# A transformer block with a mixture of experts: two thirds of the shared expert moved ahead of the experts, with the routing done at once beside it

## The chip, the cores and the metric

One Trainium2 chip, one of its cores. The metric is the device time of one execution in microseconds; several executions are taken, and their median counts. A core has five engines with instruction queues of their own: TensorE (PE: matmuls, and weight loads PEld), VectorE (DVE), ScalarE (ACT), GpSimd (POOL) and SyncE (SP, which here only issues DMAs). They wait for each other by semaphores. An engine works through its queue in order, so whatever stands behind a waiting instruction waits too.

## What is computed

The input is 32 blocks of 256 tokens with 256 features. A token mixer with a layer norm gives `h`; one class token is put ahead of each block (so 32 x 257 rows); attention with 16 heads is added. The change is in what comes then, a gated feed-forward with a shared expert of 1024 hidden columns and eight routed experts of 256, of which each row takes two:

```python
xf = layernorm(h).reshape(-1, 256)
shared = silu(xf @ shared_w1.T) * (xf @ shared_w2.T) @ shared_w3.T
scores = sigmoid(xf @ router_w.T)
_, top_idx = top_k(scores + expert_bias, 2)
gates = scores * one_hot(top_idx, 8).sum(axis=-2)
h12 = einsum('td,ehd->teh', xf, w12); h1, h2 = split(h12, 2, axis=-1)
routed = einsum('teh,edh->td', silu(h1) * h2 * gates[:, :, None], w3)
return h + (shared + routed)
```

## The kernel before

**Stage A** (`stage_a`, one block of instructions) does mixer and attention, unrolled by batch and software-pipelined over 16 places n of a step. Its `ffn_stats` (lines 812 to 825) takes mean and variance of each finished block of rows for the last layer norm into `mv3`; the blocks themselves go to `hscr` in DRAM. At the very end DVE adds epsilon to all 66 columns (L973) and POOL takes the power -0.5 of them at once (L1049).

**Stage B** (`stage_b`) is three blocks of instructions, each ended by a barrier of all engines. Rows are held as K = 33 blocks of two tiles of 128 rows (32 blocks, and one with the 32 class rows).

*Routing* goes over the 33 blocks. Per block: SP loads `hb` (L1175, L1178); DVE normalises (`norm`, L1158); PE transposes (`turn`, L1204); ACT and DVE split z into a high and a low part (L1249, L1338), since products are made of three fp32r terms; PE makes the logits with matmuls of 8 columns (`router`, L1216); ACT takes Tanh (L1253); DVE ranks the eight scores, picks two and makes the gates (`scores`, L1272 to L1292); PE counts the rows before each row (`counts`, L1226 to L1230); DVE turns that into two row numbers (`places`, L1299 to L1334); POOL writes the normalised rows to these places of `zs` with four indirect DMAs (L1433). Every expert has a region of `zs` large enough for all rows. The first 12 blocks also carry the weights: load (L1173), copy to fp32r on ACT (L1258, `whi`), subtraction on POOL (L1427, `wlo`), through two buffers. After the last block DVE makes the lists of tiles and moves all row numbers (L1375 to L1420), and POOL writes the rows of zeros that fill each expert's last tile (L1440).

*Experts* goes over NT = 140 tiles of 128 gathered rows. SP loads a tile from `zs` (L1473, its row number read from a table) and stores the result to `ys` (L1481); the four other engines are pipelined over three tiles.

*Shared expert* goes over the 33 blocks in a loop of two. Per block: z again from `hscr`, then four times (u = 0 to 3) `hidden` (24 matmuls of 256 columns, L1656), Silu (L1696), product (L1729), `head` and `split` into high and low parts (L1703, L1735), and, one u later, `output` (12 matmuls, L1670), with `turn` of the next block at u = 2. The block's sum is added to `h` (L1751); four indirect DMAs of POOL gather its expert rows from `ys` (L1790), DVE adds them times their gates (L1756), and SP stores the output (L1624).

Of the kernel before, what the change touches and what calls it, by code (L numbers as in the profile page):

```python
# [15 lines left out]
F32 = mybir.dt.float32  # L16
# [7 lines left out]
D = C * H  # L24
P = 128
# [43 lines left out]
def stage_a(nc, ctx, sem, a, hscr, mv3, rs3, eye, mhalf, ps):  # L69
# [55 lines left out]
    mh65 = sb("mh65", [P, (B + 1) * LT])  # L125
# [64 lines left out]
    wo_in, wos_ok, vb_ok, vb_in, roh_ok = sem("wo_in"), sem("wos_ok"), sem("vb_ok"), sem("vb_in"), sem("roh_ok")  # L190
# [8 lines left out]
    pcr_ok, pc_ok = sem("pcr_ok"), sem("pc_ok")  # L199
# [139 lines left out]
    def _(pe):  # L339
# [244 lines left out]
        pe.wait_ge(spread_ok, 1)  # L584
        pe.wait_ge(ones_in, 16 * 2 * 2)
        pe.wait_ge(vb_in, 16 * 3)
        pe.wait_ge(wos_ok, 1)
# [136 lines left out]
    def _(dve):  # L724
# [89 lines left out]
        def ffn_stats(b):  # L814
# [4 lines left out]
            dve.wait_ge(ln3, b * 5 + 2)  # L819
# [3 lines left out]
            dve.wait_ge(ln3, b * 5 + 4)  # L823
# [41 lines left out]
        dve.memset(mh65[:], -0.5)  # L865
# [67 lines left out]
        for n in range(2):  # L933
            for f in range(FT):
# [14 lines left out]
                          ALU.subtract).then_inc(wos_ok, 1)  # L949
# [20 lines left out]
        dve.wait_ge(ln3, 5 * B + 1)  # L970
        dve.bn_aggr(mv3[:, B * LT, :], st3[:, 0, :]).then_inc(ln3, 1)
        dve.wait_ge(ln3, 5 * B + 2)
        dve.tensor_scalar(rs3[:], mv3[:, :, 1], EPS, None, ALU.add).then_inc(ln3, 1)  # L973
# [3 lines left out]
    def _(pool):  # L977
# [68 lines left out]
        for j in range(B + 2):  # L1046
            batch(j, j)
        pool.wait_ge(ln3, 5 * B + 3)
        pool.tensor_tensor(rs3[:], rs3[:], mh65[:], ALU.pow)  # L1049


def stage_b(nc, ctx, sem, a, out, hscr, mv3, rs3, eye, ps):

# [12 lines left out]
    REG = K * L + P  # L1066
    NT = (TOP * K * L + NE * (P - 1)) // P + 1
    assert NT % 2 == 0
    UW = FT * 2 * UH + 2 * D
    ONE = LT * NE  # L1070
    zs = nc.dram_tensor("zs", [NE * REG, D], F32, kind="Internal").ap()
    ys = nc.dram_tensor("ys", [NT * P, D], F32, kind="Internal").ap()

    whi = sb("whi", [P, NU, UW], F32R)
    wlo = sb("wlo", [P, NU, UW], F32R)
    rwr = sb("rwr", [P, FT * NE])
    rwh = sb("rwh", [P, FT, NE], F32R)
    rwl = sb("rwl", [P, FT, NE], F32R)
    ebias = sb("ebias", [P, ONE])
    before = sb("before", [P, ONE, NE])  # L1080
    earlierf = sb("earlierf", [P, P])
    earlier = sb("earlier", [P, P], F32R)
    ones = sb("ones", [P, P], F32R)
    region = sb("region", [P, ONE])
    rowid = sb("rowid", [P, 1])
    tileid = sb("tileid", [1, NT])
    hb = [sb("hb%d" % p, [P, LT, D]) for p in range(2)]
    z3 = [sb("z3_%d" % p, [P, LT, D]) for p in range(3)]
# [4 lines left out]
    uu = sb("uu", [P, 3, 2 * L])  # L1093
    raw2 = sb("raw2", [P, UW])
    RAW = 2
    raw = [uu[:].rearrange("p a b -> p (a b)"), raw2[:]]
    assert UW == 3 * 2 * L
# [3 lines left out]
    th = sb("th", [P, ONE])  # L1101
    sc = sb("sc", [P, ONE])
    key = sb("key", [P, ONE])
    gt = sb("gt", [P, ONE, NE])
    eq = sb("eq", [P, ONE, NE])
    rank = sb("rank", [P, ONE])
    gate = sb("gate", [P, ONE])
    mask = sb("mask", [P, ONE], F32R)
    filled = sb("filled", [P, ONE])
    slot = sb("slot", [P, ONE])  # L1110
    smax = sb("smax", [P, LT])
    ssum = sb("ssum", [P, LT])
    hit = sb("hit", [P, TOP, ONE])
    two = sb("two", [P, LT, TOP])
    idx = [sb("idx%d" % p, [P, LT * TOP], I32) for p in range(3)]
    slots = sb("slots", [P, K * LT * TOP])
    offset = sb("offset", [P, K * LT * TOP])
    moved = sb("moved", [P, K * LT * TOP])
    shift = sb("shift", [P, NE])
    idxs = sb("idxs", [P, K * LT * TOP], I32)  # L1120
    gates = sb("gates", [P, K * LT * TOP])
    gnow = sb("gnow", [P, LT * TOP])
    tail = sb("tail", [P, NE], I32)
    tailf = sb("tailf", [P, NE])
    rows = sb("rows", [1, NT], I32)
# [744 lines left out]
```

## Time and profile before

| | us |
|---|---|
| median of the runs shown | 2719.99 (2716.59 to 2720.41, 3 runs) |
| the profiled execution | 2719.27, its span 2717.4 |
| busy: PE, PEld | 2368.3, 1952.8 |
| busy: DVE, ACT, POOL | 1541.2, 1023.1, 696.2 |
| mean granted clock of TensorE | 0.915 |

Busy time is summed by engine over the span. Matmuls are pipelined, so a busy PE is not PE at its peak. The granted clock is the share of 2.4 GHz that TensorE was given; it has two levels, 2.4 and 1.2 GHz (1.00 and 0.50), and a window that lies across a switch shows a mean.

### The profile page before, as it was taken

To read this page: it belongs to the slowest core of one execution; us is meant where nothing else is said; L and a number is where in the kernel's file an instruction comes from. 1 tells how busy PE (TensorE), PEld (TensorE's weight loads), DVE (VectorE), ACT (ScalarE), POOL (GpSimd) and SP (SyncE) were. 2 spreads that over 40 slices of the span, in tenths; PEclk is the share of its full clock that TensorE was granted. 3 is DMA by queue.
4 is the path that set the end of the run, shared out by engine and by line. 5 is a ranking of instruction groups with operands and counts; after the bars stand their busy time and mean duration, and the time that the engine had idled before them with its cause. 6 is when DMAs were issued, how large, how long until landed. Compare 5 with 4: busy or idle time off the path is not lost. (4 is left out here: it accounts for less than half of the span.)

```text
span 2717.4 us, 47912 instructions
## 1 busy us (share of the span) xinstructions
PE 2368.3 (87%) x15654; PEld 1952.8 (72%) x15655; DVE 1541.2 (57%) x3820; ACT 1023.1 (38%) x2129; POOL 696.2 (26%) x775
## 2 busy tenths in 40 slices
PE   3789999999999999998735674999999899999999
PEld 3567777677766777776424563777777799999999
DVE  5356666666666666665248886333443355555554
ACT  0144444444544454444412111444444233333332
POOL 2232223322332233221037654000000122222222
PEclk9689999999999999999755555999999999999999
DMA  2333322333233323333025332222222122222111
GB/s 69 44 52 72 66 57 58 72 66 64 52 71 71 67 51 64 73 58 57 16 77 165 121 116 85 85 85 85 85 87 85 47 62 62 62 62 60 58 57 54
DMA packets 136380, 190.30 MB, mean 70 GB/s; under 512 B 24323, under 2 KB 96021, under 8 KB 136261
## 3 DMA queue, kind: packets, MB, share of 16 engines
q1 hardware_dynamic: 123204, 153.06, 24.1%
q0 software_dynamic: 13056, 35.67, 4.0%
q8 instruction: 73, 1.20, 0.2%
q14 instruction: 47, 0.38, 0.1%
HBM read 82.06 MB, written 54.03 MB: 50 GB/s over the span
## 5 line engine op out<-in xcount | busy, mean ns | idle before, releaser
L793 DVE TENSOR_REDUCE mx<-ps 128x2 f32<-128x514 f32 x512 | 351.1, 686 | 219.4 <-PE ps L448 219.3
L633 ACT ACTIVATE pT<-ps 128x514 f32<-128x514 f32 x512 | 307.0, 600 | 377.7 <-PE ps L465 373.4
L448 PE MATMUL ps<-km,q 112*128 112x258 f32 x1024 | 265.0, 341 | 91.3 <-DVE mx L793 79.3
L448 PEld LDWEIGHTS ps<-km,q 112*128 112x128 f32 x1024 | 164.0, 193 | 188.0 <-DVE mx L793 140.3
L465 PE MATMUL ps<-q,km 114*128 114x258 f32 x1024 | 233.6, 310 | 12.4 <-ACT pT L633 8.8
L1786 POOL TENSOR_TENSOR mark<-rowid 128x1 f32<-128x1 f32 x33 | 6.4, 194 | 854.2 <-DVE idx L1742 854.2
L1656 PE MATMUL ps<-zhi,whi 128*128 128x256 f32 x1056 | 214.4, 285 | 1.5 <-DVE zlo L1724 1.5
L1656 PE MATMUL ps<-zhi,wlo 128*128 128x256 f32 x1056 | 211.1, 281 | 0.0
L1656 PE MATMUL ps<-zlo,whi 128*128 128x256 f32 x1056 | 210.7, 281 | 0.0
L465 PEld LDWEIGHTS ps<-q,km 114*128 114x128 f32 x1024 | 164.9, 196 | 61.2 <-issue 31.1
L996 POOL TENSOR_TENSOR nb<-mv,mneg 128x2 f32<-128x2 f32 x32 | 6.2, 195 | 737.8 <-DVE rs L756 737.8
L1729 DVE TENSOR_TENSOR uu<-ps,sil 128x512 f32<-128x512 f32 x132 | 91.1, 690 | 157.8 <-ACT sil L1696 138.5
L1696 ACT ACTIVATE sil<-ps 128x512 f32<-128x512 f32 x132 | 78.9, 598 | 259.2 <-PE ps L1656 259.2
L1656 PEld LDWEIGHTS ps<-zhi,whi 128*128 128x128 f32 x1056 | 163.2, 190 | 1.9 <-ACT zhi L1707 1.9
L1656 PEld LDWEIGHTS ps<-zhi,wlo 128*128 128x128 f32 x1056 | 163.0, 189 | 0.0
L1656 PEld LDWEIGHTS ps<-zlo,whi 128*128 128x128 f32 x1056 | 162.5, 189 | 0.0
L482 PE MATMUL ps<-pT,va 128*32 128x257 f32 x2048 | 146.3, 399 | 0.0
L1735 DVE TENSOR_TENSOR hlo<-uu,hhi 128x512 fp32r<-128x512 f32 x132 | 91.4, 692 | 92.2 <-ACT hhi L1703 91.5
L1790 POOL DMA_INDIRECT raw<-ys,idx x132 | 130.8, 991 | 38.1 <-issue 33.5
L1595 DVE TENSOR_TENSOR uu<-ps,sil 128x256 f32<-128x256 f32 x140 | 59.5, 425 | 142.8 <-ACT sil L1576 142.8
L1433 POOL DMA_INDIRECT zs<-z,idx x132 | 128.2, 971 | 35.3 <-issue 34.9
L734 DVE RECIPROCAL rden<-ps 128x256 f32<-128x256 f32 x64 | 112.0, 1752 | 30.2 <-PE ps L372 30.2
(326 smaller groups left out, 5459.5 us busy)
## 6 DMA issues: line engine op xcount, KB each, us to landing
z<-zs SPq DMA_DIRECT2D x140, 128.0 KB, 2.0
ys<-z SPq DMA_DIRECT2D x140, 128.0 KB, 1.8
hb<-hscr SPq DMA_DIRECT2D x66, 256.0 KB
q<-qhi SPq DMA_DIRECT2D x128, 129.0 KB, 4.2
km<-khi SPq DMA_DIRECT2D x256, 64.5 KB, 3.3
xs<-in_x SPq DMA_DIRECT2D x64, 256.0 KB, 4.6
hscr<-h SPq DMA_DIRECT2D x34, 256.0 KB, 5.1
q<-qlo SPq DMA_DIRECT2D x64, 129.0 KB, 5.1
```

The source lines that it names most:

```text
L448: last = pe.matmul(ps[:, k, 0:NP], q2[p % U][0:MAXROW, QAT[g], t * P:(t + 1) * P], km[p % 2][0:MAXROW, k, g, :], start=True, stop=True)
L465: pe.matmul(ps[:, 4 + k, 0:NP], km[p % 2][0:MAXROW + 2, k, g, t * P:(t + 1) * P], q2[p % U][0:MAXROW + 2, QAT[g], :], start=True, stop=Tru ...
L482: last = pe.matmul(ps[SLOT * j:SLOT * (j + 1), 7, 0:N], va[p % 2][:, t, h, :], pT[:, h, t, :], start=False, stop=(t == LT - 1), skip_group ...
L633: act.activation(pT[:, 2 * g:2 * g + 2, t, :], ps[:, 4:6, 0:N], ACT.Exp, scale=HD ** -0.5).then_inc(s_ok, 1)
L734: dve.reciprocal(rden[:, f, :], ps[:, 3, f * L:(f + 1) * L]).then_inc(y_step, 1)
L793: dve.tensor_reduce(mx[:, t, 2 * QAT[g]:2 * QAT[g] + 2], ps[:, 0:2, 0:N], AX_X, ALU.max, negate=True).then_inc(mx_ok, 1)
L1433: pool.indirect_dma_start(zs, bass.IndirectOffsetOnAxis(idx[p][:, at:at + 1], 0), z3[p][:, t, :], None).then_inc(zs_out[p], 16)
L1656: last = pe.matmul(ps[:, 2 * (u % 2) + c, m * L:(m + 1) * L], w_[:, u, at:at + P], z_[:, f, :], start=(n == 0), stop=(n == len(mm) - 1))
L1696: act.activation(sil[:, u % 2, :].rearrange("p (c l) -> p c l", c=2), ps[:, 2 * (u % 2):2 * (u % 2) + 2, 0:L], ACT.Silu).then_inc(sil_ok, 1)
L1729: dve.tensor_tensor(uu[:, u % 2, :].rearrange("p (c l) -> p c l", c=2), ps[:, 2 * (u % 2):2 * (u % 2) + 2, L:2 * L], sil[:, u % 2, :].rear ...
L1735: dve.tensor_tensor(hlo[:, u % 2, :], uu[:, u % 2, :], hhi[:, u % 2, :], ALU.subtract).then_inc(hlo_ok, 1)
L1790: pool.indirect_dma_start(yg[:, t, c, :], None, ys, bass.IndirectOffsetOnAxis(idx[0][:, at:at + 1], 0)).then_inc(y_in, 16)
```

## The change

Three things are changed, which the diff below shows in its core.

In stage A, `ffn_stats` now also adds epsilon for its block (one more DVE operation), and POOL takes the root of these two columns in the new `ffn_root`, four batches later in its list; only two columns are left for the end.

Stage B keeps three blocks of instructions, with other contents. The *first* computes the shared expert of 22 of the 33 blocks (XN), unrolled. Beside blocks 0 to 10 it also normalises, transposes and splits the 22 other blocks, two per block (`norm_x`, `turn_x`, `high_x`, `low_x`), makes the logits of all 33, and stores every normalised block to DRAM (`zd`). The weights of the eight experts are loaded at the ends of blocks 0 to 7. Beside blocks 11 to 15 DVE routes all rows at once with operations 520 columns wide (`route`), cut into pieces placed after each u. POOL then writes the tails and all scatters, each from one of three buffers that SP fills from `zd` (`load_s`). The sum of shared expert and h goes back to `hscr` (`store_acc`). Row numbers are now final when they are made, so `zs` is compact. The *second* is the expert stage as before, over NT = 136 tiles; SP's row number is the tile's. The *third* is the shared expert of the 11 last blocks, unrolled, with the gathers and combines of all 33 blocks, three per block, through two buffers (the 32 class rows apart).

```diff
 def ffn_stats(b):
+            dve.tensor_scalar(rs3[:, bass.ds(b * LT, LT)], mvb[:, :, 1], EPS, None, ALU.add).then_inc(ln3, 1)
...
+        def ffn_root(b):
+            pool.wait_ge(ln3, b * 6 + 6)
+            pool.tensor_tensor(rs3[:, bass.ds(b * LT, LT)], rs3[:, bass.ds(b * LT, LT)], mhalf[:], ALU.pow)
         def batch(j, p):
             if has(j + 1):
                 split_x(j + 1, p + 1)
+            if has(j - 4):
+                ffn_root(j - 4)
...
-        pool.tensor_tensor(rs3[:], rs3[:], mh65[:], ALU.pow)
+        pool.tensor_tensor(rs3[:, B * LT:], rs3[:, B * LT:], mhalf[:], ALU.pow)
...
-    NT = (TOP * K * L + NE * (P - 1)) // P + 1
+    NT = (TOP * (B * L + B) + NE * (P - 1)) // P
+    X1 = K // 3
+    XN = 2 * X1
+    NX = 3
...
+            def load_s(s):
+                if s >= NX:
+                    sp.wait_ge(zs_out[s % NX], 16 * LT * TOP * (s // NX))
+                sp.dma_start(zx[s % NX][:], zd[s]).then_inc(zx_in[s % NX], 16)
...
+            for k in range(XN):
+                if k > 0:
+                    store_acc(sp, k - 1)
+                    if k < XN - 1:
+                        load_h(sp, k + 1)
+                if k < X1:
...
+                elif k == X1:
...
+                    for s in range(NX):
+                        load_s(s)
+                elif k >= X1 + 3:
+                    per = -(-(K - NX) // (XN - X1 - 3))
+                    for s in range(NX + per * (k - X1 - 3), min(K, NX + per * (k - X1 - 2))):
+                        load_s(s)
+            store_acc(sp, XN - 1)
...
+            for k in range(XN):
+                for u in range(NS):
+                    hidden(pe, k, u)
+                    if u >= 1:
+                        output(pe, k, u - 1)
+                    elif k > 0:
+                        output(pe, k - 1, NS - 1)
+                    if k < X1:
+                        if u == 0:
+                            logits(k, k % 2)
+                            turn_x(2 * k)
+                        if u == 1:
+                            logits_x(2 * k)
+                            turn_x(2 * k + 1)
+                        if u == 2:
+                            logits_x(2 * k + 1)
+                    if u == 2 and k < XN - 1:
+                        turn(pe, k + 1)
+                if k == X1 + 1:
+                    places()
...
+            def route(k, u):
+                if (k, u) == (X1, 1):
+                    keys()
+                if (k, u) == (X1, 2):
+                    best(0)
+                if (k, u) == (X1, 3):
+                    single(0)
...
+                if (k, u) == (X1 + 1, 2):
+                    single(1)
+                    masks()
...
+                if (k, u) == (X1 + 3, 0):
+                    tables()
+                if (k, u) == (X1 + 3, 1):
+                    positions()
+                if (k, u) == (X1 + 3, 2):
+                    slots(0)
+                    slots(1)
...
+                if (k, u) == (X1 + 4, 1):
+                    lists()
...
+            def scatter(s):
+                b = s % NX
+                pool.wait_ge(zx_in[b], 16 * (held[b] + s // NX + 1))
+                pool.tensor_tensor(mark[:, s:s + 1], rowid[:], rowid[:], ALU.add)
+                rows = P if s < B else B
+                for t in range(LT if s < B else 1):
                     for c in range(TOP):
+                        pool.indirect_dma_start(zs, bass.IndirectOffsetOnAxis(idxs[0:rows, s * LT + t, c:c + 1], 0),
+                                                zx[b][0:rows, t, :], None).then_inc(zs_out[b], 16)
...
+            for e in range(NE):
+                pool.indirect_dma_start(zs, bass.IndirectOffsetOnAxis(tail[:, e:e + 1], 0), zero[:], None).then_inc(tail_out, 16)
             pool.wait_ge(tail_out, 16 * NE)
+            pool.wait_ge(idx_ok, TOP)
+            for s in range(K):
+                scatter(s)
...
+            def combine(c):
+                q = c % 2
+                dve.wait_ge(hc_in[q], 16 * (c // 2 + 1))
+                dve.wait_ge(y_in[q], 16 * LT * TOP * (c // 2 + 1))
...
+            for c in range(K):
+                q = c % 2
+                if c >= 2:
+                    pool.wait_ge(cb_ok, c - 1)
...
```

## Rows read from the trace of the kernel before

**Rows 1.** The page's head and its line of TensorE clocks, 40 slices of the span.

```profile
span 2717.4 us, 47912 instructions
...
PEclk9689999999999999999755555999999999999999
```

**Rows 2.** Windows by stage: length, busy us (xinstructions) per engine, granted clock, DMA share, GB/s.

```profile
0.00:1391.00 1391.00, 1203.59 (x7837) 908.52 (x7838) 829.25 (x1742) 599.92 (x1192) 375.39 (x425) 0.95 0.30 59
1391.00:1684.00 293.00, 161.75 (x693) 145.74 (x693) 233.44 (x1064) 42.30 (x79) 183.64 (x185) 0.50 0.39 125
1684.00:2124.00 440.00, 421.06 (x2240) 317.57 (x2240) 171.87 (x420) 198.96 (x561) 0.00 (x0) 0.99 0.27 83
2124.00:2717.00 593.00, 581.91 (x4884) 580.97 (x4884) 306.69 (x594) 181.90 (x297) 137.19 (x165) 0.99 0.20 58
```

**Rows 3.** Timeline of shared blocks: start us, us, engine, line, operation [idle before <-releaser].

```profile
2680.60 0.68 DVE L1751 TENSOR_TENSOR acc<-ps,hb 128x512 f32<-128x512 f32 x1
...
2695.43 0.60 ACT L1696 ACTIVATE sil<-ps 128x512 f32<-128x512 f32 x1 [2.29 <-PE ps L1656]
...
2697.45 0.69 DVE L1735 TENSOR_TENSOR hlo<-uu,hhi 128x512 fp32r<-128x512 f32 x1 [0.70 <-ACT hhi L1703]
...
2698.13 0.68 DVE L1751 TENSOR_TENSOR acc<-ps,hb 128x512 f32<-128x512 f32 x1
```

**Rows 4.** Timeline of the experts: the output copies of tiles two apart.

```profile
2079.98 0.38 ACT L1566 ACTIVATE z<-ps 128x256 f32<-128x256 f32 x1 [0.65 <-PE ps L1519]
...
2086.12 0.38 ACT L1566 ACTIVATE z<-ps 128x256 f32<-128x256 f32 x1 [0.65 <-PE ps L1519]
```

**Rows 5.** Timeline, POOL: the last `mark` of the routing, and the first tail after its scatters.

```profile
1661.30 0.19 POOL L1429 TENSOR_TENSOR mark<-rowid 128x1 f32<-128x1 f32 x1 [1.51 <-DVE idx L1321]
...
1666.72 0.96 POOL L1440 DMA_INDIRECT zs<-z,tail  x1 [0.30 <-issue]
```

**Rows 6.** Timeline of stage A: a root of two columns, and the stage's end.

```profile
1226.12 0.71 POOL L1009 TENSOR_TENSOR rs<-rs,mhalf 128x2 f32<-128x2 f32 x1
...
1379.76 0.20 DVE L973 TENSOR_SCALAR rs<-mv 128x66 f32<-128x66 f32 x1
1380.04 10.94 POOL L1049 TENSOR_TENSOR rs<-rs,mh 128x66 f32<-128x66 f32 x1 [47.59 <-DVE rs L973]
1391.28 0.34 SPq L1166 DMA_DIRECT2D rwr<-in_routerT  x1
```

**Rows 7.** Timeline, TensorE in stage A: four narrow matmuls, and the next group.

```profile
1249.19 0.63 PE L382 MATMUL ps<-idr,xh 128*128 128x64 f32 x4
...
1249.66 1.11 PE L385 MATMUL ps<-outw,rden 128*128 128x256 f32 x4
```

**Rows 8.** DMA issues of the routing stage: size, median us to landing.

```profile
uu<-in_wu SPq DMA_DIRECT2D x6, 768.0 KB, 4.9
```

**Rows 9.** Timeline of the routing stage: the weights' copy and subtraction, and DVE beside it.

```profile
1414.09 1.48 ACT L1258 ACTIVATE whi<-raw 128x1536 fp32r<-128x1536 f32 x1
...
1418.25 3.58 DVE L1304 TENSOR_TENSOR slot<-slot,mask 128x16 f32<-128x16 f32 x1
1418.35 3.43 POOL L1427 TENSOR_TENSOR wlo<-raw,whi 128x1536 fp32r<-128x1536 f32 x1
```

**Rows 10.** Timeline, DVE after the routing: seven chained additions of one column.

```profile
1664.31 1.34 DVE L1386 TENSOR_TENSOR upto<-upto,ntile 128x1 f32<-128x1 f32 x7
```

**Rows 11.** Timeline: the first loads of the experts and of the last stage.

```profile
1684.63 11.08 SPq L1473 DMA_DIRECT2D z<-zs  x6
...
2124.41 0.83 SPq L1628 DMA_DIRECT2D hb<-hscr  x2
```

**Rows 12.** Groups of the page: busy us, mean ns of one | idle before, and its releaser.

```profile
L1790 POOL DMA_INDIRECT raw<-ys,idx x132 | 130.8, 991 | 38.1 <-issue 33.5
...
L1433 POOL DMA_INDIRECT zs<-z,idx x132 | 128.2, 971 | 35.3 <-issue 34.9
```

**Rows 13.** A window of stage A with gaps of TensorE, columns as in rows 2.

```profile
1300.00:1320.00 20.00, 14.05 (x98) 9.60 (x96) 11.55 (x25) 9.24 (x19) 0.73 (x1) 1.00 0.07 26
```

More of the change, by code:

```diff
@@ L1116, in stage_b @@
[L1116 to L1122, printed above, removed]
+    one = [sb("hit%d" % c, [P, WIDE]) for c in range(TOP)]
+    key, tmp, sum_a, sum_b, sc = (raws[:, n * WIDE:(n + 1) * WIDE] for n in range(5))
+    mask = sb("mask", [P, WIDE], F32R)
+    top = sb("top", [P, T])
@@ new lines, in places @@
+            def places():
+                pe.wait_ge(mask_ok, 1)
+                pe.wait_ge(th_ok, 2)
+                pe.wait_ge(lo_ok3, X1 + 3)
+                pe.matmul(ps[:, 5, :], earlier[:], mask[:, 0:BANK], start=True, stop=True)
+                pe.matmul(ps[:, 7, :], ones[:], mask[:, 0:BANK], start=True, stop=True)
+                pe.matmul(ps[:, 6, 0:NE], earlier[:], mask[:, BANK:WIDE], start=True, stop=True)
+                pe.matmul(ps[:, 6, NE:2 * NE], ones[:], mask[:, BANK:WIDE], start=True, stop=True).then_inc(pos_ps, 1)
@@ L1419, in _ @@
-            chain(dve.tensor_tensor(slots[:], slots[:], offset[:], ALU.add))
-            dve.tensor_copy(idxs[:], slots[:])
+            z_low(dve, 0)
+            for k in range(XN):
+                for u in range(NS):
+                    product(dve, k, u)
+                    split(dve, k, u)
+                    if u == 0 and k > 0:
+                        total(dve, k - 1)
+                    if k < X1 and u < 2:
+                        low_x(2 * k + u)
+                    if k < XN - 1:
+                        if u == 1:
+                            z_norm(dve, k + 1)
+                        if u == 2:
+                            z_low(dve, k + 1)
+                    if u >= 2 and 2 * k + u < EXTRA:
+                        norm_x(2 * k + u)
+                    route(k, u)
@@ new lines, in store_c @@
+            def store_c(c):
+                sp.wait_ge(cb_ok, c + 1)
+                sp.dma_start(out[c, 1:N, :].rearrange("(t p) d -> p t d", p=P), hc[c % 2]).then_inc(out_d[c % 2], 16)
+            load_h(sp, XN)
+            load_h(sp, XN + 1)
+            load_c(0)
+            load_c(1)
+            at = 2
+            for k in range(XN, K):
+                if k > XN:
+                    store_acc(sp, k - 1)
+                    if k < K - 1:
+                        load_h(sp, k + 1)
+                while at < k and at - 2 <= combined(k)[-1]:
+                    store_c(at - 2)
+                    load_c(at)
+                    at += 1
@@ L1675, in blk @@
-            def blk(k, p):
-                nxt = not isinstance(k, int) or k < K - 1
+            turn(pe, XN)
+            for k in range(XN, K):
                 for u in range(NS):
-                    hidden(k, p, u)
+                    hidden(pe, k, u)
                     if u >= 1:
-                        output(k, u - 1)
-                    elif later(k):
-                        output(k - 1, NS - 1)
-                    if u == 2 and nxt:
-                        turn(k + 1)
-            turn(0)
@@ L1775, in _ @@
-            dve.wait_ge(hb3_in[0], 16)
-            norm(dve, 0, hb[0], z3[0], z_ok3)
-            pick(0)
-            z_low(0, 0)
-            blocks3(dve, blk)
-            gather(K - 1, (K - 1) % 2)
+                    if n == 0:
+                        last.then_inc(cb_step, 1)
+                        dve.wait_ge(cb_step, c + 1)
+                last.then_inc(cb_ok, 1)
+            z_norm(dve, XN)
+            z_low(dve, XN)
+            for k in range(XN, K):
+                for u in range(NS):
+                    product(dve, k, u)
+                    split(dve, k, u)
+                    if u == 0 and k > XN:
+                        total(dve, k - 1)
+                    if k < K - 1:
+                        if u == 1:
+                            z_norm(dve, k + 1)
+                        if u == 2:
+                            z_low(dve, k + 1)
+                    if u >= 1 and u - 1 < len(combined(k)):
+                        combine(combined(k)[u - 1])
```

867 lines of the change are left out of this document (431 added, 436 removed).

## The prediction, made before the changed kernel was run

> **What bounds the kernel now.** I read the page first: 2717.4 us of span, and a TensorE clock of 9 or 10 tenths everywhere but in six slices in the middle, where it is 5 to 7 [rows 1]. A table of windows cut at the stages says what that middle is [rows 2]. Attention takes 1391 us. Routing takes 293 us at a granted clock of 0.50 with TensorE busy for 162 of them. The experts take 440 us at 0.99, and the shared expert 593 us with 582 busy. So TensorE bounds the last two stages, and nothing saturates in routing: its blocks are a chain through five engines, and TensorE's work there is small. The change puts this stage under matmuls that have to be done anyway. To price that I need the period of a shared block, of an expert tile, and of POOL's scatter.
>
> Between two equal points of consecutive shared blocks lie 2698.13 - 2680.60 = 17.53 us [rows 3], all of it TensorE. Two expert tiles take 2086.12 - 2079.98 = 6.14 us, one 3.07 [rows 4]. From one `mark` of POOL to what follows its four indirect DMAs lie 1666.72 - 1661.30 = 5.42 us, one DMA every 1.27 us [rows 5].
>
> The profiled execution took 2719.27 us, 1.9 more than its span; the median of the runs shown is 2719.99. I sum against the profiled one.
>
> **Stage A.** The last root goes from 66 columns (10.94 us on POOL, nothing beside it [rows 6]) to 2, as the root of L1009, 0.71 us [rows 6]. That gives back 10.2 us. Added are one small DVE operation and one such POOL root per block, 32 times. POOL waits most of the time; `ffn_root(j-4)` stands ahead of `mixer_affine(j)`, but its input is made at n=8 and the other's at n=10 of the same step, so it delays nobody. DVE's operation adds about 0.1 to 0.2 us where DVE sometimes holds TensorE up: 0 to 6 us in all, I take 3. New start of the next stage: 1391.3 - 10.2 + 3 = 1384.
>
> **The first 11 shared blocks, with logits.** Each has its 17.53 us plus, for three row blocks, 36 matmuls of 8 columns and 8 transposes. At full clock four matmuls of 64 columns leave 0.47 us until the next group [rows 7], so I take 0.11 us each: 44 x 0.11 = 4.8, a block of 22.4 us. Bounds: nothing, if they fitted into gaps (there are none), and 0.22 each at half clock, 9.7. The casts for them go to ACT and DVE, which have room: a shared block uses 306.7/33 = 9.3 us of DVE and 5.5 of ACT [rows 2]. The order of SP (one store, up to three loads, three stores of z) waits in this stretch only for things that are made earlier in the same block.
>
> **Start of it.** Four weight units must pass load, ACT and POOL before block 0 can end: 4.9 us [rows 8], 1.48 and 3.43 [rows 9], two buffers, behind some 2.5 MB of other loads and stores. I work out unit 0 at +11, unit 1 at +21, unit 2 at +25, unit 3 at +31 us, then a hidden and an output step at the lower clock: block 1 starts at +39 us. Bounds 30 and 48.
>
> **Routing of all rows on DVE**, in blocks 11 to 14. A wide operation (520 columns) costs as the 512-column split, 0.69 [rows 3], and some 0.04 until the next. A small chained one costs 1.34/7 = 0.19 [rows 10]. After the Silu starts, DVE's split ends 2697.45 + 0.69 - 2695.43 = 2.7 us later [rows 3]; matmuls of a quarter block take 4.4. So some 2.2 us per quarter are free for DVE, and 1.3 more before TensorE waits. Keys 1.5, best 1.5, single 2.2 fit. `single(1)` with `masks` (3.3 beside `z_low`) exceeds by 0.5; `tables` (23 small ones, 4.7, beside `total`) by 2 to 3; `positions` (2.3) and `slots` (3.3) find no slack left and are late by 1 to 2 each; `lists` (5.1) by 2.4 but that one is hidden below. The indices are ready about 23 us after the start of block 14.
>
> **The scatters: the term that decides.** POOL writes 8 tails after `tables` (10.2 us and a landing, done at +23.7 us of block 14, so they set the start), then 130 DMAs: 32 x 5.42 + 2.9 = 176.3 us. Let T0 be their start: 39 + 10 x 22.4 + 3 x 17.53 + 1 + 23.7 = 340 us after the stage's start. TensorE has 7 blocks and a bit left, 130 us. So POOL, not TensorE, ends this stage, and TensorE must idle some 50 us. The code says where: from block 14 on, SP issues four `load_s` per block, each waiting for the scatter three places back, and the next block's `load_h` stands behind them in the same queue. So blocks 15 to 21 run at the pace of four scatters, 21.7 us instead of 17.5, after a first wait of about 16 us in block 15. `load_h(21)` comes after scatter 23, T0 + 132, and block 21 is over at T0 + 161, ahead of POOL's T0 + 176 + 3 for landing and the barrier. The stage lasts 340 + 179 = 519, I say 520 us.
>
> **Experts.** From first load to the first load of the next stage, 2124.41 - 1684.63 = 439.8 us [rows 11]; 136 tiles in place of 140 take 4 x 3.07 = 12.3 off: 427.5. SP no longer reads row numbers from a table; it was never late, no gain. TensorE comes cold as before.
>
> **Last stage.** 11 blocks in place of 33: 593.0 (2717.4 - 2124.4) less 22 x 17.53 = 207.3 us. It carries all 33 gathers, three per block: 16.3 us of POOL in 17.5. With two buffers the third combine of a block waits 0.6 us on its gather, within DVE's slack. Bounds 0 and 15 us; I take 2. DVE carries 7.6 + 3 x 1.9 = 13.3 us per block, enough room.
>
> **Sum:** 1384 + 520 + 427.5 + 209 + 1.9 = 2542; against 2719.3 this is -177 us: -7 in stage A, -12 tiles, -158 in what were routing and the shared expert (293 + 593 before, 729 after).
>
> **Rules weighed.** In the trace a multiplication of two small SBUF tiles on DVE takes 3.58 us while POOL's 3.43 us subtraction runs [rows 9]. After block 4's weights this can catch one `split` per block, but TensorE then has logits and transposes to do, 3 us of slack: nothing in my sum. The Trainium skill (SBUF — State Buffer, "Who interferes with whom") has this as a lock held for the whole instruction, and adds that a DVE operation in a two-port mode keeps POOL from writing DMA descriptors. By that rule every scatter beside the shared expert's DVE work could be late by such an operation; that is rival 2.
>
> **Rivals.**
> 1. *The scatters hide completely.* If a block's scatters took under 3.8 us, the stage would be TensorE's: 39 + 10 x 22.4 + 11 x 17.53 + 5 for routing + 3 at the end = 464, 56 us under mine: 2486. Against it: 132 scatters and 132 gathers both show 0.97 to 0.99 us and little spread [rows 12]. 0.08.
> 2. *POOL is slower than 5.42.* Each scatter meets one or two of DVE's 0.69 us operations, and waits for it: 6.3 us each, 33 x 0.9 = +29, 2571. Against it: POOL kept 1.27 us while DVE was busy 80% of the routing stage (233 of 293 [rows 2]); for it: that stage had mostly tiny operations. 0.15.
> 3. *Straight-line code.* The shared blocks leave their loop and become 33 unrolled ones; if TensorE's instructions came late by 2 us per block, +50 and 2590. Stage A is unrolled and ran at clock 1.00 without such gaps, but with fewer matmuls per us. 0.06. The Trainium skill (Runtime: NRT & Kernel Launch, "Instruction fetch mechanics") says that straight code streams in unseen and that a taken branch is what stalls; by it this rival costs nothing.
> 4. *Slower than before.* The granted clock stays at 0.50, as it did through all of routing [rows 2], because TensorE now waits in each block for z, logits and routing. Its 17.1 us of matmuls per block double: 22 blocks give up to +390, about 2930. It decides once some 10 blocks run so. Against it: 1.00 was granted where TensorE was busy 70% of 20 us [rows 13], and blocks 0 to 13 have hardly a gap. 0.04.
> 5. *Another wait in SP's queue or a mis-sized start*, within +-30 us of mine but in a place I don't name: 0.07.
>
> **How the numbers follow.** My own case has 0.60, with terms from 2515 to 2575. Rivals 1 to 3 stand from 2486 to 2590; 2480 to 2605 takes in their places and leaves out under 2 in 10. This kernel's measurement can tell 0.2%, 5.4 us, from no change. All cases but rival 4 are faster by far more; I give faster 0.94, same 0.01, slower 0.05.
>
> **What would show it.** Right: POOL's first scatter near 1725 us, 130 of them in a row at 1.27 us until about 1901; TensorE busy near 100% until about 1740, then 80%, SP waiting in `load_s` for POOL's DMAs; the experts' first load near 1904 and the last stage's near 2331. Wrong: no gap of TensorE in blocks 15 to 21 (rival 1), longer POOL intervals (2), TensorE idle with nothing waited for (3), or clock 0.50 in the window 1430 to 1700 (4).

## The result, and the profile after

The changed kernel takes 2564.6 us (median; 2559.9 to 2568.8, four executions) against 2718.3 beside it: a ratio of 0.9435, 95% interval [0.9414, 0.9457]. The forecast was 2542. The profiled execution took 2562.4 us, its span 2559.6. So 154 us were gained where 177 were forecast. In the profiled execution the last stage took 27 us more than forecast and stage A 10 less; the rest of the sum came within 2 us:

| | before | forecast | after |
|---|---|---|---|
| first load after stage A, at | 1391.3 | 1384 | 1374.1 |
| from there to the experts' first load | 293.4 | 520 | 521.5 |
| experts | 439.8 | 427.5 | 427.8 |
| last stage | 593.0 | 209 | 236.3 |
| outside the span | 1.9 | 1.9 | 2.8 |

The windows of the changed kernel, cut at its stages (length, busy us of each engine, granted clock, DMA share, GB/s, as in [rows 2]):

```profile
0.00:1374.00 1374.00, 1196.32 (x7837) 901.66 (x7838) 830.86 (x1773) 600.69 (x1192) 387.22 (x457) 0.96 0.30 60
1374.00:1896.00 522.00, 448.60 (x3738) 445.51 (x3738) 232.25 (x421) 152.04 (x237) 187.46 (x184) 0.92 0.36 122
1896.00:2323.00 427.00, 408.40 (x2176) 307.89 (x2176) 166.99 (x408) 193.16 (x544) 0.00 (x0) 0.99 0.26 84
2323.00:2559.60 236.60, 200.72 (x1628) 194.12 (x1628) 134.46 (x262) 59.24 (x99) 140.27 (x163) 0.97 0.55 167
```

Compare the last line with that of [rows 2]. There TensorE was busy 582 of 593 us; here it is busy 201 of 237, while the DMA engines carry 167 GB/s instead of 58. The last stage is no longer TensorE's alone. The first one, which replaces the 293 us of routing at half clock, has TensorE busy 449 of 522 us and a clock of 0.92.

The scatters went as forecast. POOL's timeline, with the idle time before each instruction and what ended it:

```profile
1706.70 0.20 POOL L1632 TENSOR_TENSOR mark<-rowid 128x1 f32<-128x1 f32 x1 [123.12 <-DVE tail L1514]
...
1718.89 0.72 POOL L1620 TENSOR_TENSOR mark<-rowid 128x1 f32<-128x1 f32 x1 [1.52 <-DMA zs<-zero,tail]
...
1891.11 0.87 POOL L1624 DMA_INDIRECT zs<-z,idxs  x1 [0.30 <-issue]
```

They start 344.8 us after the stage's first load (forecast 340) and take 173 us (forecast 176). The next view is DVE's timeline: the sum of block 14, and the norm in block 15.

```profile
1723.16 0.68 DVE L1253 TENSOR_TENSOR acc<-ps,hb 128x512 f32<-128x512 f32 x1
...
1748.08 0.74 DVE L1151 TENSOR_SCALAR z<-hb,mv,rs 128x256 f32<-128x256 f32 x2 [21.14 <-DMA hb<-hscr]
```

The 21.1 us are the wait that was forecast as "about 16". SP stood in `load_s`, with the next `hb` behind it, as its timeline shows:

```profile
1726.80 15.85 SPq L1282 DMA_DIRECT2D z<-zd  x4
1742.69 0.45 SPq L1160 DMA_DIRECT2D hscr<-acc  x1
1743.19 0.43 SPq L1156 DMA_DIRECT2D hb<-hscr  x1
```

The sum of block 15 comes at 1764.8, 41.6 us after that of block 14, and the next five follow at 17.1 to 23.8 us, 20.2 in the mean (forecast 21.7). That of block 21 ends at 1880.9, T0 + 162 by the measured T0 of 1718.9 (forecast T0 + 161). TensorE has then nothing left to do in this stage until POOL is through.

In the last stage the chain of waits is new. The waits of all engines in the window 2340 to 2550 (engine, line, what ended the wait: us in total, times, longest):

```profile
ACT hhi L1219 <- DVE uu L1239: 101.3, 40, 5.0
...
POOL mark L1919 <- DVE raws L1876: 47.8, 11, 8.0
...
DVE z L1151 <- DMA hb<-hscr: 37.1, 9, 5.1
...
DVE raws L1876 <- DMA raws<-ys,idxs: 16.1, 10, 2.2
```

DVE stands 4 us in each block at the norm, waiting for the load of `hb`. It works in order, so products and combines behind it are late, ACT waits for the product (first row), and POOL waits for the combine before it may gather again (second). DVE's timeline of one block shows where the wait comes from:

```profile
2416.05 0.68 DVE L1253 TENSOR_TENSOR acc<-ps,hb 128x512 f32<-128x512 f32 x1
2416.66 0.68 DVE L1239 TENSOR_TENSOR uu<-ps,sil 128x512 f32<-128x512 f32 x1
2418.04 0.69 DVE L1245 TENSOR_TENSOR hlo<-uu,hhi 128x512 fp32r<-128x512 f32 x1 [0.70 <-ACT hhi L1219]
2423.31 0.73 DVE L1151 TENSOR_SCALAR z<-hb,mv,rs 128x256 f32<-128x256 f32 x2 [4.58 <-DMA hb<-hscr]
2423.97 1.79 DVE L1876 SCALAR_TENSOR_TENSOR raws<-raws,gates 128x256 f32<-128x256 f32 x4
```

And SP's, in the same block:

```profile
2417.35 0.32 SPq L1816 DMA_DIRECT2D raws<-hscr  x1
2417.72 0.43 SPq L1160 DMA_DIRECT2D hscr<-acc  x1
2418.19 0.43 SPq L1156 DMA_DIRECT2D hb<-hscr  x1
```

The total frees the buffer at 2416.7. SP was still held by a load for the combine (`raws`), which it issued at 2417.35; then come the store of the sum and, behind it, the load of `hb` at 2418.19. DVE was ready for the norm at 2418.7. The DMA issues of the window 2340 to 2550, with the median from issue to landing, in this trace and in that of the same kernel measured once more:

```profile
hb<-hscr SPq DMA_DIRECT2D x9, 256.0 KB, 5.1
...
hb<-hscr SPq DMA_DIRECT2D x9, 256.0 KB, 4.1
```

Of the landing only what exceeds the cover is a wait, 37.1 us in nine blocks here and 31.9 in the second trace. In the kernel before, the same buffer turned round in the same place without any wait. Timelines of its DVE and its SP tell why:

```profile
2610.55 0.68 DVE L1751 TENSOR_TENSOR acc<-ps,hb 128x512 f32<-128x512 f32 x1
2611.27 1.79 DVE L1756 SCALAR_TENSOR_TENSOR acc<-raw,gnow,acc 128x256 f32<-128x256 f32 x4
...
2615.04 0.73 DVE L1158 TENSOR_SCALAR z<-hb,mv,rs 128x256 f32<-128x256 f32 x2
...
2611.43 0.34 SPq L1621 DMA_DIRECT2D hb<-hscr  x1
```

A combine stood between total and norm and put 3.8 us between them instead of 2.0; SP issued the load 0.2 us after the total, not 1.5; and the DMA engines moved a third of the bytes per second.

### The profile page after: what moved, and what is told of

Its sections match the earlier page's. It is cut to its first block and busy times, and to the rows that moved or that the text cites. A ratio compares the mean times of both kernels' runs of the same rounds, so it can differ in the third digit from the quotient of the medians.

```text
span 2559.6 us, 44029 instructions
## 1 busy us (share of the span) xinstructions
PE 2254.0 (88%) x15379; PEld 1849.2 (72%) x15380; DVE 1364.5 (53%) x2864; ACT 1005.1 (39%) x2072; POOL 714.9 (28%) x804
## 5 line engine op out<-in xcount | busy, mean ns | idle before, releaser
L1026 POOL TENSOR_TENSOR rs<-rs,mhalf 128x2 f32<-128x2 f32 x32 | 22.3, 696 | 547.0 <-DVE mv L823 547.0
L1219 ACT ACTIVATE hhi<-uu 128x512 fp32r<-128x512 f32 x132 | 83.4, 632 | 222.2 <-DVE uu L1239 186.6
L1245 DVE TENSOR_TENSOR hlo<-uu,hhi 128x512 fp32r<-128x512 f32 x132 | 96.8, 734 | 92.1 <-ACT hhi L1219 92.1
L1923 POOL DMA_INDIRECT raws<-ys,idxs x130 | 131.9, 1014 | 37.1 <-issue 34.8
L1624 POOL DMA_INDIRECT zs<-z,idxs x130 | 129.3, 994 | 34.8 <-issue 34.8
L1203 PE MATMUL ps<-whi,hhi 128*128 128x256 f32 x528 | 108.7, 288 | 32.9 <-DVE hlo L1245 18.1
```

Of the source, the lines that this page charges most:

```text
L1203: last = pe.matmul(ps[:, 4, t * D:(t + 1) * D], h_[:, u % 2, c * L + t * P:c * L + (t + 1) * P], w_[:, u, at:at + D], start=(n == 0 and u ...
L1219: act.activation(hhi[:, u % 2, :], uu[:, u % 2, :], ACT.Copy).then_inc(hhi_ok, 1)
L1245: dve.tensor_tensor(hlo[:, u % 2, :], uu[:, u % 2, :], hhi[:, u % 2, :], ALU.subtract).then_inc(hlo_ok, 1)
L1624: pool.indirect_dma_start(zs, bass.IndirectOffsetOnAxis(idxs[0:rows, s * LT + t, c:c + 1], 0), zx[b][0:rows, t, :], None).then_inc(zs_out[ ...
L1923: pool.indirect_dma_start(yg[q][0:rows, t, n, :], None, ys, bass.IndirectOffsetOnAxis(idxs[0:rows, c * LT + t, n:n + 1], 0)).then_inc(y_in ...
```

## The experiments

The theory (T) was this loop: two buffers of `h`, a load that can only start at the total, a landing that is longer than what covers it. Its rivals were POOL's three gathers per block (U) and the work that DVE itself has to do in a block (V). A second question was what ends the first stage. Every median below has the kernel before measured beside it, at 2715.9 to 2718.7.

| kernel | median us | last stage us |
|---|---|---|
| changed kernel, again | 2563.6 | 232.2 |
| load ahead of store | 2555.2 | 226.6 |
| third buffer of `h` | 2536.9 | 208.3 |
| third buffer of the combine | 2551.0 | 223.4 |
| both buffers | 2528.0 | 202.2 |
| no gathers | 2535.4 | 209.4 |

"Last stage" is from the first load of `hb` to the end of the span of the profiled execution. In the five traces in which this stage is unedited it is 232.0 to 237.0, so differences under 5 us there mean nothing. In the same five the norm waits 31.9 to 37.1 us in nine blocks (the stage's first wait, 6.6 to 7.1 us, left out), and the load of `hb` lands after 4.1 to 5.2 us in the median.

**Load ahead of store** in the last stage.

```diff
                 if k > XN:
-                    store_acc(sp, k - 1)
+                    sp.wait_ge(acc_ok, k)
                     if k < K - 1:
                         load_h(sp, k + 1)
+                    store_acc(sp, k - 1)
```

> Base: the changed kernel, 2562.4 us profiled, 2564.6 median; its last stage lasts 236.3 us instead of the 209 forecast. Only the last stage is edited: when a block's total is there, SP issues the load of the next block's h ahead of the store of the sum, instead of behind it. Theory T (loop through the two buffers of h: the load can start only after the total at u=0, 5.1 us to landing, and DVE stands at the norm 3.2 to 4.6 us in each block, in order, so the three combines, their stores and gathers shift too): the load is issued 0.5 us earlier and has less traffic beside it; the wait shrinks by 1 us or more per block, total -5 to -15, I say 2556. Rival U (the three gathers per block on POOL set the period, 16.3 us plus the wait for a combine): nothing, 2562 to 2564. Rival V (DVE's own load of combines): nothing either.

The ratio is 0.9397 [0.9380, 0.9414], 9 us under the changed kernel. The norm's wait fell to 23.7 us in nine blocks, 0.9 to 1.5 us per block. The load is issued 0.5 us earlier; the rest is a shorter landing, 3.9 us in the median. That lies only just under the 4.1 to 5.2 of the unedited stage, so whether the store's new place shortened it isn't shown.

**Third buffer of `h`**, loaded two blocks ahead.

```diff
+    h3 = [hb[0], hb[1], one[0][:, 0:LT * D].rearrange("p (t d) -> p t d", t=LT)]
...
-                    if k < K - 1:
-                        load_h(sp, k + 1)
+                    if k + 2 < K:
+                        load_h(sp, k + 2)
```

> Only the last stage is edited: a third buffer of h, and the load goes two blocks ahead, so that no norm has to wait for it. Gathers, combines and their two buffers as before. Theory T: the 43.8 us that DVE waits at the norm in 10 blocks vanish, the period falls from some 20.5 to 18 to 18.5 us, last stage 213 to 218, total 2541 to 2546. Rival U (POOL's gathers): the wait only moves to the third combine of a block, which then waits 4 us instead of 1.6; last stage 233 or more, total at most 3 us less. Rival V (DVE load): 16 us of work per block fit in 17.5; as T.

The buffer is a tile that only the routing uses. Ratio 0.9341 [0.9318, 0.9364], 28 us under the changed kernel, more than T asked for. The only wait left at the norm is the stage's first, 6.8 us. The gathers' waits stayed, though, in the waits of this kernel between 2340 and 2520:

```profile
POOL mark L1928 <- DVE raws L1885: 19.0, 10, 8.3
DVE raws L1885 <- DMA raws<-ys,idxs: 13.3, 10, 2.4
```

DVE waits as often and nearly as long for gathered rows as before (16.1), and the stage is at 208.3. U is out as the cause of these 28 us. What its wait does cost shows two runs further on.

**Third pair of buffers for the combine** (`yg` and `hc`), `h` with two as before.

```diff
-            for c in range(K):
-                q = c % 2
-                if c >= 2:
-                    pool.wait_ge(cb_ok, c - 1)
+                q = c % G
+                if c >= G:
+                    pool.wait_ge(cb_ok, c - G + 1)
```

> Only the last stage is edited: a third pair of buffers for gathered rows and h in the combine, h's own two buffers as they were. POOL then runs one gather further ahead. Theory T: the 16 us that DVE waits for gathers vanish, but the load of h still starts at the total, so the norm still waits 3 to 5 us per block: total -5 to -12, 2552 to 2559, and the wait for hb in the trace stays near 40 us. Rival U: POOL becomes free, last stage 210 to 214, total 2538 to 2542.

Ratio 0.9393 [0.9368, 0.9418], 14 us under the changed kernel. The stage is 9 to 14 us shorter. That is 1 us past T's range and 9 us short of U's. The norm's wait is still 30.3 us in nine blocks, as T has it, and DVE waits no longer for gathered rows.

**Both.**

> Both of the two edits before together: third buffer of h loaded two blocks ahead, and third pair of buffers for the combine. Theory T: TensorE's pace, 17.5 us per block, last stage 207 to 211 as the prediction had it, total 2534 to 2539. Rival U: POOL still needs 16.3 us per block plus DMA congestion (its descriptors land later while 165 GB/s move), last stage 215 or more. Rival V (DVE carries 16 us per block and comes late at the Silu products): 215 to 222.

Ratio 0.9311 [0.9292, 0.9330], and 202.2 us, under what T and the forecast had as TensorE's own time. It is 6 us less than with the third buffer of `h` alone, so with two gather buffers POOL's gathers cost these 6 us. The sums in this stage:

```profile
2352.60 0.68 DVE L1262 TENSOR_TENSOR acc<-ps,hb 128x512 f32<-128x512 f32 x1
...
2369.72 0.68 DVE L1262 TENSOR_TENSOR acc<-ps,hit 128x512 f32<-128x512 f32 x1
```

They come every 17.12 us, nine in a row to the hundredth. A block of this kernel takes 17.12 us where one of the kernel before took 17.53 [rows 3]; why its loop was 0.41 slower wasn't tried. V is out: DVE is busy for the same 135 us in this stage, and ACT's wait for its products, over the whole stage, fell from 102.8 to 18.9 us.

**No gathers.** POOL issues none, DVE waits for none, and the combines add zeros times gates, so the experts' part is missing from the output. `h` has its two buffers.

```diff
-                        pool.indirect_dma_start(yg[q][0:rows, t, n, :], None, ys, ...)
...
-                        last = dve.scalar_tensor_tensor(out=hc[q][:, t, :], in0=yg[q][:, t, n, :],
+                        last = dve.scalar_tensor_tensor(out=hc[q][:, t, :], in0=zero[:],
```

> Last stage without its 130 indirect DMAs: POOL issues none, and the combines add zeros times gates, so the experts' part is missing in the output; all waits of POOL on combines, all combines, loads and stores stay, and h has its two buffers. Theory T as it now stands after the third buffer of h (last stage 208.3) and the gather buffer beside it (202.2): the load of h cannot start before the total, and 5.1 us of landing do not fit into the 3.6 us until the norm; the gathers' traffic is what makes the landing 5.1. Without them it lands in 2.5 to 3.5 us and the norm waits under 1 us: last stage 202 to 207, total 2528 to 2535. Rival (the landing is slow by itself, store and combine loads beside it): the norm still waits 3 us or more, last stage 215 or more.

The result lies between the two: 2535.4, 209.4 us, a landing of 3.7 us, and at the norm between 2340 and 2530:

```profile
DVE z L1151 <- DMA hb<-hscr: 15.3, 9, 3.1
```

So 1.7 us of wait per block are there without gathers, and 1.8 to 2.4 come with them. Of these, 0.4 to 1.5 us are a longer landing (108 GB/s moved in this stage, 166 to 170 with gathers); and SP, less often held up by the combine's buffers, issued six of nine loads 0.4 to 0.5 us after the total where 1.1 is usual. Both causes are real, a load that starts too late and what the gathers add to it. This run doesn't split the second one further.

**What ends the first stage.** SP's loads for the scatters start a block later, three per block, with nine left for the end.

```diff
-                elif k >= X1 + 3:
-                    per = -(-(K - NX) // (XN - X1 - 3))
-                    for s in range(NX + per * (k - X1 - 3), min(K, NX + per * (k - X1 - 2))):
+                elif k >= X1 + 4:
+                    for s in range(NX + 3 * (k - X1 - 4), NX + 3 * (k - X1 - 3)):
                         load_s(s)
             store_acc(sp, XN - 1)
+            for s in range(NX + 3 * (XN - X1 - 4), K):
+                load_s(s)
```

> Only SP's list in the first stage is edited: the loads for the scatters begin one block later (block 15) and come three per block, not four, so that the load of the next block's h never waits for a scatter for long; the 9 that are left over come behind block 21. Theory T (POOL's 33 scatters of 5.3 us end the stage, and TensorE's 50 us of idleness are only placed inside blocks 15 to 21 by SP's order): TensorE runs blocks 15 to 21 at 17.5 us without gaps, block 21 is over near 1843 to 1848 instead of 1880, TensorE is then idle some 50 us, scatters end near 1892 as before, total unchanged, 2560 to 2567. Rival (the waits in SP's queue are themselves on the path): the stage shortens by 10 or more, total 2554 or less.

2567.4 us, ratio 0.9451 [0.9429, 0.9472]: no gain. TensorE's last sum comes at 1844.8 instead of 1880.2, and it then stands still (windows of this kernel, columns as in [rows 2]):

```profile
1760.00:1800.00 40.00, 40.00 (x348) 40.00 (x347) 17.82 (x29) 12.68 (x21) 30.94 (x37) 1.00 0.51 173
1800.00:1840.00 40.00, 40.00 (x348) 40.00 (x347) 16.62 (x27) 12.05 (x20) 30.18 (x36) 1.00 0.52 174
1840.00:1880.00 40.00, 3.22 (x26) 2.85 (x24) 2.08 (x3) 1.23 (x2) 31.77 (x39) 0.61 0.47 155
```

POOL is busy at the same rate throughout (fifth engine column) and ends the stage after 523.7 us; three waits for its own loads, 3.1 us together, are new. The idleness of TensorE is POOL's doing; SP's order only says where it lies.

**A 23rd block for that idle time**, with both buffers and this order of SP.

```diff
-    XN = 2 * X1
+    XN = 2 * X1 + 1
```

> Third buffer of h, third pair for the combine, SP's order of the first stage as in the run with three loads per block, and 23 instead of 22 blocks in the first stage (10 instead of 11 in the last). Theory T: POOL's scatters still end the first stage, so the 23rd block is hidden in TensorE's 50 idle us; last stage 202.2 - 17.5 = 185 if TensorE sets it, 33 x 5.42 + 8 = 187 if POOL's gathers do: total 2509 to 2514 in place of 2528. Rival 1 (TensorE's blocks end the first stage after all): it grows by up to 17.5 us and the total stays at 2528. Rival 2 (the last stage is now POOL's, and its congestion with 3.3 gathers per block costs 5 to 10 us): 2518 to 2522.

2527.7 us, ratio 0.9299 [0.9281, 0.9318], no better than both buffers alone. The block is hidden, as T says: the sum of the 23rd comes at 1866.1, before the last scatter at 1900.2. But the last stage fell to 192.7 us only, not 185. Its sums come every 17.1 us up to the last, which comes 21.7 us after the one ahead of it where 14.5 is usual, because the last combine stands before it on DVE and waits for its gathered rows:

```profile
2520.25 1.80 DVE L1891 SCALAR_TENSOR_TENSOR raws<-raws,gates 128x256 f32<-128x256 f32 x4 [3.47 <-DMA raws<-ys,idxs]
2521.96 0.68 DVE L1262 TENSOR_TENSOR acc<-ps,hit 128x512 f32<-128x512 f32 x1
```

So this stage now ends with POOL's gathers, which is the mechanism of rival 2, though the total is rival 1's. The first stage took 525.2 us instead of 518.9, some of which is SP's order (523.7 in the run before), and this execution's stage A ended 4 us later. A block moved is worth some 3 us net, which these intervals can't tell from nothing.

**An earlier start of the scatters.** Both buffers, and the routing on DVE packed into blocks 11 and 12 (the diff shows part of the list). With it the counting matmuls come one place earlier, and SP's loads for the scatters three per block from block 13 on.

```diff
                 if (k, u) == (X1, 1):
                     keys()
+                    best(0)
                 if (k, u) == (X1, 2):
-                    best(0)
+                    single(0)
+                    rest()
...
-                if (k, u) == (X1 + 3, 0):
                     tables()
-                if (k, u) == (X1 + 3, 1):
+                if (k, u) == (X1 + 1, 3):
                     positions()
-                if (k, u) == (X1 + 3, 2):
                     slots(0)
                     slots(1)
```

> Third buffer of h and third pair for the combine as in the run at 2528; SP's loads for the scatters three per block from block 13 on; and the routing on DVE packed into blocks 11 and 12 (two or three pieces after each u, where they took blocks 11 to 14 one or two at a time), with its counting matmuls one place earlier. Theory T (the start of the scatters plus their 173 to 176 us set the first stage, TensorE has 50 us to spare): the table is ready some 18 us earlier (range 15 to 22), TensorE loses 10 to 20 us of its spare time to DVE and nothing of the total; first scatter at 326 us of the stage instead of 345, stage 503 instead of 521, total 2510 (2505 to 2515). Rival 1 (TensorE's own work ends the stage once it has these stalls): block 21 ends after the last scatter, total 2518 or more. Rival 2 (packed 520-column pieces meet something else, so that the table is not earlier): 2526 to 2530.

2515.3 us, ratio 0.9254 [0.9233, 0.9275], the fastest kernel of this study. Its POOL:

```profile
1688.59 0.19 POOL L1636 TENSOR_TENSOR mark<-rowid 128x1 f32<-128x1 f32 x1 [105.50 <-DVE tail L1524]
...
1698.81 0.96 POOL L1638 DMA_INDIRECT zs<-zero,tail  x1 [0.30 <-issue]
1702.76 0.19 POOL L1624 TENSOR_TENSOR mark<-rowid 128x1 f32<-128x1 f32 x1 [2.98 <-DMA zs<-zero,tail]
```

The table is there 314.5 us after the stage's first load instead of 332.6, 18 us earlier as expected; two of these go to tails that take longer. The stage takes 507.3 us; in the traces with this stage unedited it took 517.0 to 521.5. The last sum of TensorE comes at 1858.3, still ahead of the last scatter at 1877.0. Less was gained than expected (13 us of 18 in the median), the mechanism is T's.

**This routing without the buffers.** The changed kernel with the last edit alone, its last stage untouched.

> The changed kernel with only the packed routing and SP's order of the run before, its last stage untouched (two buffers of h, two pairs for the combine). Theory T: the two gains add, since one stage ends in a barrier before the other: last stage 236 as it was, total 2564.6 - 18 = 2547 (2542 to 2552). Rival: TensorE or the barrier takes the 18 us back, 2557 or more.

2547.5 us, ratio 0.9370 [0.9349, 0.9390], 16 under the changed kernel measured beside it (below). The gains of the two stages add.

**The changed kernel again**, beside the last two.

> The changed kernel itself, unedited, once more beside the next two. Every theory expects 2560 to 2569. In its trace: scatters begin 345 us after the first stage's first load and take 173 us, last stage 236 us; stage A's end anywhere between 1372 and 1384, as in the traces so far.

2563.6 us, ratio 0.9430 [0.9412, 0.9449]. The scatters begin 343.8 us after the first load and take 172.4; the last stage takes 232.2, and stage A ends at 1380.8. So the ends of stage A lie 7 us apart, and the last stages 4, in two executions of one and the same kernel.

**The root of stage A put back**, and the roots per block left out.

```diff
-        pool.tensor_tensor(rs3[:, B * LT:], rs3[:, B * LT:], mhalf[:], ALU.pow)
+        pool.tensor_tensor(rs3[:], rs3[:], mh65[:], ALU.pow)
```

> Only stage A's root is put back: no root per block, and at the end one of POOL over 66 columns, as in the kernel before; the extra DVE operation per block stays. Theory T: the last root takes 10.9 us instead of 0.7, nothing beside it, so the total rises by 10.2, to 2573 to 2577. The next stage had started 17.2 us sooner in the changed kernel's trace than in the one of before, 7 more than the root explains. Rival 1: these 7 are the change's too (roots spread over POOL relieve someone): total +17, 2580 or more. Rival 2: the scatter of stage A between executions: +10 as T, and the starts of the next stage in these traces differ by several us.

2573.5 us, ratio 0.9466 [0.9449, 0.9484]: 9 to 10 us more. From the last store of stage A to the next stage's first load it is 12.2 us instead of 2.5. Rival 2 holds: the other 7 us don't come from the roots (last section).

**The cover put back**: the first combine of a block ahead of the norm, as in the kernel before.

```diff
+                    if u == 1 and len(combined(k)) > 0:
+                        combine(combined(k)[0])
                     if k < K - 1:
                         if u == 1:
                             z_norm(dve, k + 1)
...
-                    if u >= 1 and u - 1 < len(combined(k)):
+                    if u >= 2 and u - 1 < len(combined(k)):
```

> The changed kernel, with two instructions groups of DVE swapped in the last stage: the first combine of a block comes ahead of the norm of the next block's z, not behind it. In the kernel before, a combine (1.79 us) stood between the total and that norm, and the norm never waited; the change moved it behind. Both buffers of h, SP's order and the gathers stay. Theory T (what was lost is the cover for the landing of h): the wait at the norm falls by the combine's 1.8 us, from 4.5 to about 2.7 us per block, and the combine's end comes earlier by as much, so that POOL's next gather starts earlier; last stage 220 to 228 instead of 232 to 237, total 2552 to 2558. Rival U (the gathers set the combines): the combine itself now waits for its rows, no gain, 2562 or more. Rival W (TensorE then waits longer for its transposes, since z comes later): slower, 2567 or more.

2657.6 us (2645.9 to 2667.7), ratio 0.9774 [0.9743, 0.9804], 93 us above the changed kernel. Its profiled execution lost 59 to 63 us in the first stage (580.2 us), from block 14 on, where its instructions are those of the changed kernel, and 32 to 37 in the last (268.8); the experts took their 428.8. TensorE's timeline in the first stage:

```profile
1742.76 0.40 PE L1203 MATMUL ps<-wlo,hhi 128*128 128x256 f32 x2
1761.91 1.11 PE L1171 MATMUL ps<-eye,z 128*128 128x128 f32 x4 [18.75 <-issue]
```

DVE and ACT show such gaps with no releaser as well. They come in the two stretches in which POOL's indirect DMAs run beside the unrolled shared blocks, which in the twelve other traces went without them. The kernel ran on a chip that none of the other runs used, but the kernel before took 2715.9 us there, as everywhere. What makes the gaps stays open, and so does how much the moved combine alone would give back. One row speaks for T, the norm's wait between 2410 and 2650, which was 31.9 to 37.1 us in the unedited stage:

```profile
DVE z L1151 <- DMA hb<-hscr: 2.6, 3, 1.0
```

With gaps elsewhere giving the load more time, that isn't proof.

## Why the prediction was right, and where its sum was off

**What bounds it, and the order of the stages:** right in kind and place. POOL's scatters end the first stage, TensorE idles in blocks 15 to 21, SP's `load_s` is what holds it there, and the experts lose 12 us.

**Stage A** (forecast 1384, measured 1374.1). The 10.2 us of the root are right. The 3 us for the added operations are not to be seen: the second trace of the changed kernel, at the clock of the kernel before, ended the stage at 1380.8, where 1391.3 less the root is 1381.1. The other 7 us of the profiled execution are luck.

**First stage** (520 against 521.5), where luck helped: a sum of errors that cancel. Block 1 starts 50 us after the first load, not 39: the four weight units were ready at +11, +22, +25 and +32, as worked out, but the first Silu stands behind their copies in ACT's queue and starts at +30. The blocks with logits take 21.3 to 22.0 us, not 22.4: the 44 small instructions cost 44 x 0.11 as forecast, on a block of 17.12. The routing pieces cost 0.2, 1.4, 0 and 4.4 us in blocks 11 to 14, near the forecast. The tails do set the start: the indices were ready at 1717.4, the last tail's landing at 1718.9. A scatter of four DMAs took (173.1 - 2.9) / 32 = 5.32 us, not 5.42 (the 33rd has two).

**The failed step** is the last stage's: "With two buffers the third combine of a block waits 0.6 us on its gather, within DVE's slack. Bounds 0 and 15 us; I take 2." On the sum's own base of 207.3 us the term measured 25 to 30 us, outside its bounds. The gather's wait was there (1.6 us) and, with the other wait gone, cost 6 us, within the bounds. What was not in the list is the load of `hb`. The prediction read the order of SP's queue for the first stage only and took the period of the kernel before as a given; in it a load landed between total and norm, beside a combine that the change moves away. Two rows would have raised the question, the load's issue and the norm 3.6 us later. With both buffers the stage takes 202.2, so with this one term at zero the kernel is at 2528, and the forecast's 2542 lies between. Of the 7 us under the forecast's 209, some 4.5 are the shorter block (11 x 0.41) and 2 the term itself.

**The rivals.** What came is rival 5, a wait in a place that wasn't named, at 27 us of its 30. Rival 1 is out, the scatters end the stage. Rival 2 is out as a cost: the scatters took 5.32 us each. Its mechanism is there on a small scale, since nine of the 130 DMAs took 1.15 to 1.47 us instead of 0.96, each beside a DVE operation, 3 us in all. The Trainium skill (SBUF — State Buffer, "Who interferes with whom") speaks, for DVE's two-port modes, of a lock held for a whole instruction; this trace shows no such delay worth a term. Rival 3: TensorE was busy 200.0 of 200 us between 1440 and 1640, in the changed kernel and all its edits. Waits without a releaser at the weight loads of its hidden matmuls come to at most 3.5 us in all, but to 65.4 in the last run, with one of 19 us at the transposes, as rival 3 describes. The Trainium skill (Runtime: NRT & Kernel Launch, "Instruction fetch mechanics") has such code stream in unseen; the hidden matmuls of the twelve other traces agree, and no run shows whether the gaps of the last one are waits for code. The clock did come back (0.92 in the first stage), so rival 4 is out.

## What to carry to other kernels

A period read from the old kernel carries the old kernel's covers with it. When work is moved between two instructions of a queue, list every transfer that was issued before and used after the gap, and ask whether it still lands in what is left; here a third buffer, in a tile that lay idle, gave 28 us. And where one serial engine ends a stage, move its start before moving anyone else's work: 18 us of earlier routing gave 13, a block moved under the scatters gave next to nothing, since the stage that it left then ended with another serial list.

## What the runs showed of the hardware

The end of stage A differs by 10 us and more between executions of the same instructions, and the granted clock of the first 400 us tells which way. In the traces of the changed kernel and its edits it was 0.95 where the next stage began at 1372.6 and twice at 1374.1, 0.94 at 1375.2 and 1375.4, 0.93 at 1377.4, 0.92 at 1379.3 and 1379.5, and 0.91 at 1379.5, 1380.8 and 1382.4; in the last run 0.89 and 1388.1. The kernel before had 0.91, and 1391.3 less the root's 10.2 is 1381.1. So the profiled pair, one near each end, shows 7 us that the change did not make.

The load of `hb`, 256 KB, landed after 4.1 to 5.2 us (medians of nine) in the five traces of the unedited last stage, which moved 166 to 170 GB/s, and after 3.7 us without the gathers at 108 GB/s. The spread among the five, of one and the same list of instructions, is nearly as large as the effect.

Most indirect DMAs of POOL took 0.96 us. In the first stage of the changed kernel 11 of the 138 took 1.15 to 1.47, and all 11 ran beside an operation of DVE; of the 46 in whose first 0.9 us DVE stood still none did.
